# A decoder layer on one core: the first stacks by halves of heads, the second row's stack behind the first keys and values, and x loaded inside a stack

## What is computed

```python
x = layernorm(x) + pos_emb[:S]
w = x.reshape(B, nW, 128, 16, 16)                       # two windows of 128 tokens in each row
local = softmax(w @ w.T / 4) @ w                        # in each window and head
comp = conv1d(x, conv_w, stride 4)[:, :64] + conv_b     # 64 compressed tokens
gt = concat([comp, global_memory])                      # and 64 global ones
glob = softmax(x @ gt.T / 4) @ gt
mix = sigmoid(concat([local, glob]) @ gate_w + gate_b)
out = (mix * local + (1 - mix) * glob) @ out_w + out_b  # is added to x
```

## Time and profile before

| | |
|---|---|
| median of 3 runs | 1131.45 us (1128.77 to 1132.52) |
| the profiled execution | 1135.56 us, span 1133.7 us |
| busy in the span | PE 1067.4 us (94%), DVE 666.5 (59%), ACT 648.2 (57%), POOL 555.9 (49%) |
| mean granted clock of PE | 0.989 of full speed |
| moved by DMA | 130.22 MB, 115 GB/s over the span |

### The profile page before, as it was taken

How to read it: one execution, slowest core, us unless ns; L and a number is a source line. 1 busy time by engine, 2 the same in 40 slices (tenths; PEclk the granted TensorE clock), 3 DMA queues, 4 the chain that set the end, 5 groups by cost and what they waited for, 6 DMA issues and landing times.

```text
span 1133.7 us, 28505 instructions
## 1 busy us (share of the span) xinstructions
PE 1067.4 (94%) x11049; PEld 915.9 (81%) x11049; DVE 666.5 (59%) x1317; ACT 648.2 (57%) x872; POOL 555.9 (49%) x678
## 2 busy tenths in 40 slices
PE   7899999999999987999999998999999999999995
PEld 6677777787777765777777776889899999999995
DVE  4488887888888875788888887423324222222221
ACT  2466666566665653777777776444455444444441
POOL 5534455353554222443566566366754544444442
PEclk9899999999999998999999999999999999999999
DMA  8564653636436332566675668564432233332222
GB/s 216 163 183 110 154 141 91 185 102 175 113 99 178 84 100 49 149 188 172 133 178 139 158 181 260 153 137 52 43 54 48 47 48 50 49 52 48 47 43 24
DMA packets 174562, 130.22 MB, mean 115 GB/s; under 512 B 60810, under 2 KB 162927, under 8 KB 174432
## 3 DMA queue, kind: packets, MB, share of 16 engines
q1 hardware_dynamic: 155280, 106.79, 35.1%
q0 software_dynamic: 15840, 18.77, 11.5%
q10 hardware_dynamic: 3312, 2.85, 0.9%
HBM read 88.29 MB, written 40.08 MB: 113 GB/s over the span
## 4 chain that ended last, share of the span: by engine, by line
PE 52%; DVE 2%; ACT 2%; issue 2%; another core or an unknown queue 2%; DMA 1%; POOLq 0%; ACTq 0%; DVEq 0%
PE ps_scores L1926 21%; PE ps_out L1944 10%; PE ps_turn L1789 5%; PE ps_misc L1821 3%; PE ps_out L1801 2%; PE ps_scores L1776 2%; PE ps_misc L1742 2%; PE ps_misc L1809 2%; PE ps_turn L1905 1%; PE ps_scores L1769 1%; PE ps_misc L1815 1%; PE ps_scores L1850 1%; ACT weights L2121 1%; PE ps_turn L1831 1%
## 5 line engine op out<-in xcount | busy, mean ns | idle before, releaser
L1926 PEld LDWEIGHTS ps_scores<-xgT,weights 128*128 128x128 f32 x2272 | 263.9, 192 | 8.3 <-ACT xgT L2145 5.0
L1926 PE MATMUL ps_scores<-xgT,weights 128*128 128x128 f32 x2272 | 266.0, 275 | 4.0 <-ACT xgT L2145 4.0
L2422 DVE TENSOR_TENSOR gate<-ps_scores,silu 128x512 f32<-128x512 f32 x71 | 49.1, 692 | 246.8 <-ACT silu L2161 222.3
L915 ACT ACTIVATE weights<-ps_scores 128x1024 f32<-128x1024 f32 x128 | 126.8, 1024 | 78.7 <-PE ps_scores L608 63.9
L2161 ACT ACTIVATE silu<-ps_scores 128x512 f32<-128x512 f32 x71 | 42.4, 598 | 209.3 <-PE ps_scores L1926 189.6
L1944 PE MATMUL ps_out<-w2s,gate 128*128 x560 | 132.6, 380 | 0.8 <-DVE y L2428 0.8
L2154 ACT COPY weights<-weights 128x2048 f32 x68 | 130.0, 1911 | 0.7 <-issue 0.2
L1944 PEld LDWEIGHTS ps_out<-w2s,gate 128*128 128x128 f32 x560 | 100.9, 190 | 12.0 <-issue 1.2
L1081 DVE TENSOR_REDUCE sa_rowmax<-ps_turn 128x8 bf16<-128x1024 f32 x64 | 77.8, 1216 | 33.9 <-PE ps_turn L585 33.9
L920 ACT CAST weights<-ps_scores 8x1024 bf16<-8x1024 f32 x64 | 64.4, 1006 | 53.3 <-PE ps_scores L599 53.3
L1611 POOL DMA_INDIRECT table<-entry,slot_i x64 | 65.0, 1016 | 37.2 <-issue 13.8
(11 more groups left out here) (307 smaller groups left out, 2096.9 us busy)
## 6 DMA issues: line engine op xcount, KB each, us to landing
weights<-w_scr SPq DMA_DIRECT2D x60, 256.0 KB, 4.2
weights<-q_scr SPq DMA_DIRECT2D x96, 128.0 KB
ks<-w_scr SPq DMA_DIRECT2D x24, 256.0 KB, 3.7
weights<-k_scr SPq DMA_DIRECT2D x48, 120.0 KB
w_scr<-wp SPq DMA_DIRECT2D x7, 768.0 KB, 3.6
q_scr<-qp SPq DMA_DIRECT2D x14, 384.0 KB
weights<-in_w1T SPq DMA_DIRECT2D x10, 512.0 KB
weights<-in_w3T SPq DMA_DIRECT2D x10, 512.0 KB
```

Of the source, the lines that this page charges most:

```text
L915: act.activation(probs[s % 2][:], m.scores[s % 2][:], ACT.Exp, scale=SCALE).then_inc(exped, 1)
L1926: mm = pe.matmul(h_ps[r % 2][:, j, c, :], weights[:, j, k, c * P:(c + 1) * P], xgT[r % 2][:, k, :], start=(k == 0), stop=(k == DT - 1))
```

## The change

- `load_first_slots` is replaced by `load_first_heads` and `load_first_tokens`, which load a slot for one half of the heads: half f is heads 8f to 8f + 7. PE waits for row 0's half 0 ahead of unit 0, for the tokens' half 0 ahead of unit 1, for half 1 ahead of units 2 and 3.
- At the start, SP issues 9 of half 0's 12 slots and 10 of half 1's, ACT the others. ACT stores the tokens and loads all six slots of their half 0; the tokens' half 1 is shared, three slots each.
- The tokens of pair 0 are split by DVE (`split_first_g`), not POOL. `g_scr` is laid out by partitions, so that a store writes runs twice as long, and `load_g` reads it so.
- Row 1's store (`store_first_pair(1)`) goes behind all of row 0's loads, and `store_keys_values(0)` ahead of row 1's stack.
- `load_x(p + 1)` moves from ahead of `stack_w(p)` to between its query slots and its key slots.
- POOL waits for `rest_in` and adds the output's bias for rows 0 to 2 at the end of row 0's round, no longer ahead of it.
- PE runs fewer filler matmuls (6, 6, 4, 10, 18 for 14, 8, 4, 16, 24), and `turn_g(0)` goes ahead of `turn_c(0)`. On ACT `copy_cT(0)` goes behind `first_g(0)`; on DVE the ones of `gs[0]` go ahead of the bias of the convolution, those of `gs[1]` behind `maxima(0, 0)`.

The diff, cut to its core:

```diff
-    g_scr = [nc.dram_tensor(f"g_scr{i}", [3, D, GK], BF16, kind="Internal").ap() for i in range(2)]
+    g_scr = [nc.dram_tensor(f"g_scr{i}", [3, P, DT, GK], BF16, kind="Internal").ap() for i in range(2)]
...
-    def load_first_slots(queue, dst, scratch, parts, loaded, slots):
+    def load_first_heads(queue, f, dst, scratch, parts, loaded, slots):
         for s in slots:
-            queue.dma_start(dst[s:KS:SLOTS], scratch[parts[s]].rearrange("(h d) t -> d h t", d=HD))\
-                .then_inc(loaded[s % 3], 16)
+            queue.dma_start(dst[s:KS:SLOTS, f * HU:(f + 1) * HU, :],
+                            scratch[parts[s], f * P:(f + 1) * P, :].rearrange("(h d) t -> d h t", d=HD))\
+                .then_inc(loaded(s), 16)
+
+    def load_first_tokens(queue, f, loaded, slots):
+        for s in slots:
+            queue.dma_start(gs[0][s:KS:SLOTS, f * HU:(f + 1) * HU, :],
+                            g_scr[0][K_PARTS[s], :, f, :].rearrange("(h d) t -> d h t", d=HD)).then_inc(loaded(s), 16)
...
             stack(qs[i].rearrange("k h r t -> k h (r t)"), w_scr[i], Q_PARTS, w_stacked, 64 * p, False)
+            if p < NP - 1:
+                load_x(p + 1)
             stack(ks[i].rearrange("k h r t -> k h (r t)"), w_scr[i], K_PARTS, w_stacked, 64 * p + 32, True)
...
         store_first_pair(0, row0_stored)
-        stack_first_row()
+        sp.wait_ge(row0_stored, 16)
+        load_first_heads(sp, 0, first_qs, first_row, Q_PARTS, heads_of_row0(0), range(SLOTS))
+        load_first_heads(sp, 0, first_ks, first_row, K_PARTS, heads_of_row0(0), range(3, SLOTS))
+        load_first_heads(sp, 1, first_qs, first_row, Q_PARTS, heads_of_row0(1), range(SLOTS))
+        load_first_heads(sp, 1, first_ks, first_row, K_PARTS, heads_of_row0(1), range(4))
+        sp.wait_ge(g_stored, 16)
+        load_first_tokens(sp, 1, heads_of_g(1), range(3))
         store_first_pair(1, w_stored)
-        store_g(0)
-        load_first_g()
...
+        store_keys_values(0)
         stack_second_row()
-        store_keys_values(0)
         load_ctx(2)
         for p in range(1, NP):
-            if p < NP - 1:
-                load_x(p + 1)
             stack_w(p)
...
-        split_g(0)
         split_k(0)
...
-        pool.wait_ge(rest_in, N_REST)
-        pool.tensor_scalar(gate_b[:], gate_b[:], 0.5, None, ALU.mult).then_inc(bias_set, 1)
-        for c in range(3):
-            add_out_bias(c)
...
+            if b == 0:
+                pool.wait_ge(rest_in, N_REST)
+                pool.tensor_scalar(gate_b[:], gate_b[:], 0.5, None, ALU.mult).then_inc(bias_set, 1)
+                for c in range(3):
+                    add_out_bias(c)
...
-        load_first_slots(act, ks[0][:, :, 0, :], first_row, K_PARTS, row0_stacked, range(4))
-        copy_cT(0, whole_out)
+        load_first_heads(act, 0, first_ks, first_row, K_PARTS, heads_of_row0(0), range(3))
         copy_gT(0)
         first_g(0)
+        copy_cT(0, whole_out)
+        act.wait_ge(g_split, 3)
+        act.dma_start(g_scr[0].rearrange("c p k t -> p c k t"), gp[:]).then_inc(g_stored, 16)
...
         act.wait_ge(g_stored, 16)
-        load_first_slots(act, gs[0][:], g_scr[0], K_PARTS, g_stacked, range(3, SLOTS))
+        load_first_tokens(act, 0, heads_of_g(0), range(SLOTS))
+        load_first_heads(act, 1, first_ks, first_row, K_PARTS, heads_of_row0(1), range(4, SLOTS))
+        load_first_tokens(act, 1, heads_of_g(1), range(3, SLOTS))
```

More of the change, by code:

```diff
@@ L232, in self_attention @@
     x_t = a["x"].rearrange("b (n p) d -> p (b n) d", p=P)
-    def load_first_slots(queue, dst, scratch, parts, loaded, slots):
+    def load_first_heads(queue, f, dst, scratch, parts, loaded, slots):
         for s in slots:
-            queue.dma_start(dst[s:KS:SLOTS], scratch[parts[s]].rearrange("(h d) t -> d h t", d=HD))\
-                .then_inc(loaded[s % 3], 16)
+            queue.dma_start(dst[s:KS:SLOTS, f * HU:(f + 1) * HU, :],
[5 more added lines that the diff above has]
+                            g_scr[0][K_PARTS[s], :, f, :].rearrange("(h d) t -> d h t", d=HD)).then_inc(loaded(s), 16)
     first_row = w_scr[0][:, :, 0:S]
+    first_qs, first_ks = qs[0][:, :, 0, :], ks[0][:, :, 0, :]
+    heads_of_row0 = lambda f: lambda s: row0_stacked[f]
+    heads_of_g = lambda f: lambda s: g_stacked[s % 3] if f else row0_stacked[2]
+    FIRST_HEADS, FIRST_GLOBAL = 2 * SLOTS * 16, SLOTS * 16
     def sync_program(sp):
@@ L261, in store_first_pair @@
                 .then_inc(stored, 16)
[L263 to L266, removed]
         def stack_second_row():
@@ L272, in stack_second_row @@
             stack(ks[0][:, :, 1, :], rows, K_PARTS, w_stacked, 32, True)
-        def load_first_g():
-            sp.wait_ge(g_stored, 16)
-            load_first_slots(sp, gs[0][:], g_scr[0], K_PARTS, g_stacked, range(3))
         def stack_w(p):
@@ L296, in store_g @@
                     sp.wait_ge(loaded, 32 * p)
-            sp.dma_start(g_scr[i].rearrange("c (k p) t -> p c k t", p=P), gp[:]).then_inc(g_stored, 16)
+            sp.dma_start(g_scr[i].rearrange("c p k t -> p c k t"), gp[:]).then_inc(g_stored, 16)
         def load_g(p):
@@ L303, in load_g @@
                 sp.wait_ge(shifted, R * UPR * (p - 1))
-            stack(gs[i][:], g_scr[i], K_PARTS, g_stacked, 32 * p, False)
+            for s, part in enumerate(K_PARTS):
+                if s > 2:
+                    sp.wait_ge(g_stacked[s % 3], 32 * p + 16)
+                sp.dma_start(gs[i][s:KS:SLOTS].rearrange("d (k h) t -> d k h t", k=DT),
+                             g_scr[i][part].rearrange("(h d) k t -> d k h t", d=HD)).then_inc(g_stacked[s % 3], 16)
         def load_ctx(c):
@@ L560, in scores @@
             i = p % 2
-            if s == 0 and b == 0:
-                for loaded in row0_stacked:
-                    pe.wait_ge(loaded, 64)
+            if b == 0 and s in (0, 2):
+                pe.wait_ge(row0_stacked[f], FIRST_HEADS)
             elif s == 0:
@@ L578, in queries_scores @@
             i = p % 2
-            if s == 1:
+            if b == 0 and s == 1:
+                pe.wait_ge(row0_stacked[2], FIRST_GLOBAL)
+            elif s == (1 if b else 3):
                 for loaded in g_stacked:
@@ L704, in tensor_program @@
         pe.wait_ge(first_in, N_FIRST)
-        keep_warm(14)
+        keep_warm(6)
         turn_w(0, m.misc)
-        keep_warm(8)
+        keep_warm(6)
         turn_w(1, side[1])
@@ L715, in tensor_program @@
             compress(0, k)
+        turn_g(0)
         turn_c(0, whole_out)
-        turn_g(0)
         pe.wait_ge(kv_in, 2 * 16)
@@ L720, in tensor_program @@
         pe.wait_ge(dve_set, 1)
-        keep_warm(16)
+        keep_warm(10)
         scores(0, 0)
-        keep_warm(24)
+        keep_warm(18)
         for b in range(NB + 1):
@@ L1138, in split_first_row, with ones_of_g, split_first_g @@
             dve.tensor_tensor(wp[:, 2, :, 0, :], rest[:], wp[:, 1, :, 0, :], ALU.subtract).then_inc(w_split, 1)
+        def ones_of_g(i):
+            dve.tensor_copy(gs[i][KS:, :, :].rearrange("j (f h) g -> j f h g", f=DT),
+                            m.ident[KS:KX_ROWS, KS:KX_ROWS].unsqueeze(1).unsqueeze(3).broadcast_to((HU, DT, HU, GK)))\
+                .then_inc(dve_set, 1)
+        def split_first_g():
+            dve.wait_ge(g_first, 1)
+            dve.tensor_tensor(grest[:], gT[:], gp[:, 0, :, :], ALU.subtract).then_inc(g_split, 1)
+            dve.wait_ge(g_split, 1)
+            dve.tensor_copy(gp[:, 1, :, :], grest[:]).then_inc(g_split, 1)
+            dve.wait_ge(g_split, 2)
+            dve.tensor_tensor(gp[:, 2, :, :], grest[:], gp[:, 1, :, :], ALU.subtract).then_inc(g_split, 1)
         normalise(0)
@@ L1147, in vector_program @@
         dve.tensor_scalar(m.neg_ident[:], m.ident[:], -1.0, None, ALU.mult).then_inc(dve_set, 1)
+        ones_of_g(0)
+        add_conv_bias(0)
+        split_first_g()
         dve.wait_ge(conv_in, N_CONV)
@@ L1151, in vector_program @@
             dve.tensor_copy(vg[i][g, :, 0:HD], memory[g, :].rearrange("p (h d) -> p h d", d=HD)).then_inc(dve_set, 1)
[L1152 to L1156, removed]
         maxima(0, 0)
+        ones_of_g(1)
         apply_norm(2)
```

## The result

The changed kernel takes **1171.16 us** (median of 4 runs, 1170.01 to 1172.66) against 1131.99 us for the kernel before on the same chip (4 runs, 1128.77 to 1134.66). The ratio is **1.0348**, with a 95% interval of 1.0318 to 1.0379. The forecast was 1172 us, in a range of 1146 to 1184. The profiled execution took 1172.66 us with a span of 1170.8, against 1135.56 and 1133.7 before: 37.1 us more.

The account below looks back on a forecast made before the run. PE, busy 96 of 100 us, was taken to set the pace in the steady rows. 1135.6 - 6.1 + 26.0 - 0.8 + 1.5 + 19.8 = 1176.0, so 1172 us against the runs' median; range 1146 to 1184.

Parts of the forecast that it names:

- The start: Row 0 to row 3's normalisation: earlier token scores on PE and no POOL hold-up, together -6.1 us (-1 to -8.5).
- row 3's normalisation: On DVE at the start: POOL no longer waits for `out_w` ahead of row 3's deviation, a gain of 1.5 us.
- the later key slots and `gs` of each pair cost nothing: Self-attention loads behind x: they come some 3 us later, their readers 3.7 or more, so zero cost.
- rival 2: Self attention: x lands in time and only the start's gain counts, 1125 us, faster; chance 9%.
- rival 3: Whole kernel: start's gain goes in the second row's late stack and x is hidden, about 1131 us; chance 4%.
- The waits: Self attention, pairs 1 to 6: DVE stalls on late x, 26.0 us (21.2 to 29.0), plus 1.5 at pair 1.
- pair 1's late store: SP's queue: second row's slots land no earlier than 50, so the split waits; +1.5 us (0 to 3.5).
- the landing of x: Load of x behind three query slots in flight: taken as 5.5 us, 4.7 at least, at most 6.0.
- The slack: PE's `subtract_max` behind DVE's maximum: 0.14 us of slack at each stall, -0.8 us over six.
- The clock: Behind each of six stalls PE's clock falls to 0.50 for 6.8 us: 3.3 us each, +19.8 us.
- of which PE is the bound in 96%: Clock term: half of 6.8 us at the lower clock, weighted by PE's 96%, gives 3.3 us a stall.
- an estimate of 3.2 us: Landing of x's 512 KB by 2.0 us plus bytes over 436e3; forecast would be near 1158 us; set aside for the trace.

Follow-up runs that it names:

- 12 repeats: Changed kernel with PE repeating the eight token matmuls for unit 3 twelve times more in rows 1, 3, 5, 7, 9, 11; 1177.36 us, ratio 1.0313.
- the second run: The changed kernel itself, unaltered, on the chip of another batch of runs; 1183.39 us, ratio 1.0351 to the kernel before.
- six repeats: Changed kernel with PE repeating the eight token matmuls for unit 3 six times more in rows 1, 3, 5, 7, 9, 11; 1176.19 us, ratio 1.0266.
- x alone: Kernel before with only load_x(p + 1) moved between the halves of the stack, the start as before; 1183.91 us, ratio 1.0362.

## Why the prediction was right

The mechanism is the forecast's: six waits of DVE on x, PE behind each, and a lower clock behind them. That the time came out 1 us from the forecast is luck: the two large terms were off by about 6 and 7 us in opposite directions, and the two profiles differ by another 5.8 us in a part that the change does not touch.

- **The start: -6.1 forecast, -5.2 measured.** DVE wanted x of pair 2 at 59.33 (67.95 less its wait of 8.62), where it read it at 64.57 before. PE's first token scores came at 32.12, forecast 31.6, and POOL no longer held up row 3's normalisation. As a gain by itself the step was wrong, though: with x back in its place it was worth nothing. The sentence that the later key slots and `gs` of each pair cost nothing failed for pair 1 once PE came earlier than its tokens. The prediction compared SP's delays with the old times of their readers, and the start had moved these. That rival 2 would give 1125 us was wrong for the same reason: rival 3 named the right outcome for a hidden x.
- **The waits: 27.5 forecast (26.0, and 1.5 for pair 1's late store); 34.1 measured.** Six, on DVE, with PE behind each: as said. For pair 1 it is 8.6 us, forecast 7.6: against the old times DVE came 5.2 us earlier and the issue 2.7 (62.50 for 65.16), a lateness of 2.5 us for which 1.5 had been put. The other five are 25.5 us, forecast 19.9, and there the landing of x was the mis-sized value: 5.5 was taken, 6.0 called the most, and three of them took 7.2 to 7.8 us; the other two took 4.6 and 4.7. The landings account for 4.2 of the 5.6 us. The tile `xres` between 50 and 420 us, against the earlier trace rows:

```profile
DMA to landing us min/median/max: 4.6/6.3/7.8
```

- **The slack: -0.8 forecast**, 0.6 measured: 0.12 to 0.13 us at five of the stalls, none at the first.
- **The clock: 19.8 forecast, about 14 worked out.** From DVE's first want of x (59.33) to the cross attention it is 419.1 us, 370.9 before; less the waits of 34.1, 14.1 are left. PE's busy time in the six windows above is 30.3 us at the lower level, and half of that is 15.1. By the profile with 12 repeats some 10 us of it hang on the pauses. The step that failed is "of which PE is the bound in 96%": the clock has already fallen while PE still stands (the windows 287 to 289 us below), and in the four stretches behind the waits of 5.4 us and more PE is busy for 48 to 60% of the time only. Row 0's fall of the clock, 6.8 us long before, is gone; the prediction had that in the range of the start, not in its sum, and its worth lies inside the -5.2.
- **Behind the self attention: 0 forecast, -5.8 between these two profiles, within the spread of one kernel's executions.** The difference is 42.9 us at the beginning of the cross attention and 37.1 at the end. But the rest of the program, from DVE's first read there to the end of the span, takes 692.4 us in this profile and 701.6 in that of the same kernel run again, whose span is 1181.9 us:

```profile
480.27 0.75 DVE L2288 BATCH_NORM_STATS2 xstats<-xres 128x6 f32<-128x256 f32 x2 [0.32 <-PEq L1234]
```

  It is 698.2 us in the kernel before, and 692.4 to 702.4 over all ten profiles. So the 5.8 us are not shown to come from the change. The medians differ by 39.2 us on this chip and by 42.7 on the one of the second run.
- **The Trainium skill**, page "DMA: Bandwidth & Descriptors", section "Anatomy of one DMA — SWDGE (gpsimd) path", whose fit made an estimate of 3.2 us for x's 512 KB: the page states it for DMAs issued by GpSimd, and this load is issued by SP. No landing here was that short; the shortest is 4.6 us, the median 6.3.

The sum by these terms is -5.2 + 34.1 + 14 - 5.8 = 37.1 us, forecast 40.4. It closes because the 14 is what is left of the same positions; the half of PE's busy time, 15.1, is the check on it. What would have shown the forecast wrong did not occur: the wait of `bn_stats` on x is there six times. From one read of a pair's rows to the next it is 53.0 to 58.6 us, 55 forecast. The sum of the waits lay outside the 25 to 30 us that the prediction gave, and three of the six outside its 3.5 to 8 us.

## What to carry to other kernels

A load that is wanted by a fixed time is judged by its issue time plus its landing behind what is then in flight, against its reader; moved behind the store and six loads, it lost a lead of up to 28 us and became six stalls, and the stalls cost about 40% on top through the clock, as far as these traces tell. Where a start gets faster, every chain that feeds the next stage must get faster with it: list the next thing each engine reads, and reckon its arrival against the new time of the reader, not the old. The same holds for a store whose source is to be written again: moved back, it stopped ACT and with it PE. And when a profile says that an engine stands still often, some useless work in the pause can tell whether the clock has a share.

## What the runs showed of the hardware

- The same 512 KB load of x took 4.6 to 7.8 us to land in the changed kernel, and up to 8.1 in the kernel with 12 repeats. What makes the long ones is open. In the three long cases here (7.2 to 7.8 us) one packet of the instruction queue ran on one DMA engine while x was under way, but in the longest it was over by 285.6 us, some 3 us before x had landed, and in the change run again the same load, issued at 62.66, took 6.9 us with no such packet between issue and landing. So that packet does not explain them.
- Ahead of the landing read at 288.87 the DMA engines' share fell, and the clock was at its lower level while PE had not started again:

```profile
287.00:288.00 1.00, 0.00 (x0) 0.00 (x0) 0.00 (x0) 0.00 (x0) 0.00 (x0) 0.50 0.94 217
288.00:289.00 1.00, 0.00 (x0) 0.00 (x0) 0.14 (x1) 0.00 (x0) 0.00 (x0) 0.50 0.19 54
```

  In the last microsecond the engines moved 54 GB/s of the 217 of the one before, and PE and DVE stood until x was complete.
- PE's pause of 2.94 us at 179.12 was followed by eight matmuls at full clock (0.62 us) and a stretch at the lower level only from 180.6 on; pauses of 5.3 to 10.1 us were followed by it at once, the one of 2.98 us at 232.43 too. The pause that six repeats cut to 2.13 us was followed by one instruction at full clock and then still by 3.4 us at the lower level; the one of 2.43 us under twelve repeats by none. In x alone a pause of 3.41 us, at 295.50, was followed by full clock first. In these runs the length of a pause alone does not tell whether the clock falls.
